# Scores first on TensorE, and column-order norms and coordinates fetched by DMA, in a fused attention and nearest-neighbour kernel

## The reference

```
q, k, v = projections of ctx; scores = q.k / 4 + mask bias   (inside each chunk of 64)
out = (softmax(scores) . v) W_out + b_out, times the mask, plus x, then normalised over the tokens
```

```
pd[n, m] = 2 p_n.p_m - |p_n|^2 - |p_m|^2 ; idx = top_k(pd, 30)
```

## Time and profile before

| | |
|---|---|
| Median of 3 runs | 6893.18 us (6890.46 to 6906.41) |
| Profiled execution, its own time | 6878.53 us |
| Its span in the trace | 6876.1 us |
| Mean granted TensorE clock | 0.894 |
| First stage, 0 to 5075 us: DVE busy | 4784.22 us |
| the same: PE busy | 4401.15 us |
| the same: POOL busy | 4301.12 us |
| the same: ACT busy | 3863.60 us |

### The profile page before, as it was taken

The page is one execution under the profiler, slowest core; times in us unless marked ns, Lnnn a source line. Parts: engine busy times, 40 slices in busy tenths (PEclk is TensorE's granted clock), DMA queues, the critical chain, the costliest instruction groups (busy, mean ns, idle before and its releaser), DMA issues. The chain is left out here.

```text
span 6876.1 us, 226732 instructions
## 1 busy us (share of the span) xinstructions
PE 5928.1 (86%) x84308; PEld 3577.8 (52%) x84308; DVE 6084.7 (88%) x8460; ACT 4455.0 (65%) x17112; POOL 4813.1 (70%) x4750
## 2 busy tenths in 40 slices
PE   8888888888888888888888888888857949999999
PEld 4555555545454555455545555555532327767776
DVE  7999999999999999999999999999976578777876
ACT  6777777777777777777777777777741543333333
POOL 6788888888888888888888888888870013333332
PEclk9988988889888888888888888889868979999999
DMA  1222222222222222222222222222223003332322
GB/s 34 75 71 84 80 78 71 78 71 78 71 87 80 78 72 83 80 77 71 77 71 77 72 75 92 73 76 83 70 95 72 0 22 85 84 92 80 91 80 76
DMA packets 245853, 508.79 MB, mean 74 GB/s; under 512 B 155868, under 2 KB 169436, under 8 KB 210780
## 3 DMA queue, kind: packets, MB, share of 16 engines
q1 hardware_dynamic: 244700, 493.37, 22.7%
HBM read 377.93 MB, written 65.01 MB: 64 GB/s over the span
## 5 line engine op out<-in xcount | busy, mean ns | idle before, releaser
L653 ACT ACTIVATE prob<-SC,row_max 128x64 f32<-128x64 f32 x6144 | 1830.1, 325 | 1080.2 <-DVE row_max L998 1037.2
L769 POOL TENSOR_TENSOR k_bd<-k_t,head_mask 128x512 f32<-128x512 f32 x1536 | 1700.6, 1128 | 7.4 <-POOL dist_row L747 4.5
L653 ACT ACTIVATION_READ_ACCUMULATOR prob<-SC,row_max 128x1 f32 x6144 | 1336.8, 218 | 0.0
L982 DVE FIND_INDEX8 nbr<-top,dist 128x8 uint16<-128x1024 f32 x1024 | 1234.5, 1217 | 0.0
L978 DVE MAX8 top<-dist 128x8 f32<-128x1024 f32 x1024 | 1192.8, 1205 | 12.2 <-DVE y_b L1021 9.9
L780 POOL TENSOR_TENSOR prob<-prob,row_rec 128x512 f32<-128x512 f32 x768 | 813.0, 1059 | 544.0 <-DVE row_rec L1006 543.3
L553 PE MATMUL SC<-k_bd,q_t 128*64 128x256 f32 x6144 | 923.8, 426 | 0.0
L980 DVE MATCH_REPLACE8 dist<-top,dist 128x1024 f32<-128x1024 f32 x768 | 923.4, 1206 | 0.0
L561 PE MATMUL PT<-ident,prob 128*128 128x128 f32 x3072 | 543.7, 304 | 401.5 <-ACT prob_t L660 396.2
L1780 DVE TENSOR_TENSOR d_oh_a<-lo,iota_a 128x4096 bf16<-128x4096 bf16 x256 | 583.8, 2291 | 245.8 <-PE DM L1632 245.6
L1673 ACT ACTIVATE dense<-DM 128x512 f32<-128x512 f32 x512 | 305.4, 597 | 756.5 <-PE DM L1632 756.2
(11 more groups left out here) (201 smaller groups left out, 10825.7 us busy)
## 6 DMA issues: line engine op xcount, KB each, us to landing
low_all<-low_scratch SPq DMA_DIRECT2D x256, 1024.0 KB, 5.1
placed<-compact SPq DMA_DIRECT2D x256, 192.0 KB, 3.8
ctx<-in_ctx SPq DMA_DIRECT2D x32, 512.0 KB, 4.1
mask<-in_mask SPq DMA_DIRECT2D x32, 512.0 KB, 7.3
xb<-in_x SPq DMA_DIRECT2D x32, 512.0 KB, 4.8
x_scratch<-xb SPq DMA_DIRECT2D x32, 512.0 KB, 5.0
y_scratch<-y_b SPq DMA_DIRECT2D x32, 512.0 KB, 6.6
d_x<-x_scratch SPq DMA_DIRECT2D x32, 512.0 KB, 5.0
```

What stands on the lines that cost most here:

```text
L653: last = act.activation(prob[:, s % 4, g * CHUNK:(g + 1) * CHUNK], SC[:, s % 2, g * CHUNK:(g + 1) * CHUNK], ACT.Exp, bias=row_max[:, s % 2 ...
L769: last = pool.tensor_tensor(k_bd[:, q % KEY_BUFS, ch, :].rearrange("p (h k) -> p h k", h=8), kk, hm, ALU.mult)
L982: last = dve.max_index(nbr[:, uu % BPB, t, k * 8:(k + 1) * 8], best, row)
```

## The change

Four edits, all in the first stage.

1. In PE's `step` the block of the scores moves ahead of the projections, the squares and the distance block. Nothing in the block itself changes.
2. The third use of the squares (h = 2, 16 matmuls) and its two copies on ACT go, with `perm3` and the semaphore `col_ready`. A batch then has 26 uses of `PJ` and not 27. ACT's copy of `PD` has no factor 2 any more, and `xcol` holds -|p|^2/2.
3. SP gets two new pieces. `columns_out` at step 17 waits for the two copies of `vrow`, stores one row of `vrow` (4 KB) to DRAM, and issues three loads that bring the coordinates from `ctx` in DRAM into `pts`, each of 1024 single values of 4 bytes spread over 128 partitions. `columns_in` at step 19 waits for the store and loads `xcol`, again 1024 single values. Both also run once before the first step.
4. ACT waits for `xcol` before the first `PD` copy of a batch, and before it overwrites `vrow` it waits for the store of the batch before. POOL's `split_row` waits for the `vrow` copies in place of `col_ready`, and `make_table` waits for the three loads.

```
-XX_AT = {8: (0,), 16: (1, 2)}
+XX_AT = {8: (0,), 16: (1,)}
+COLS_OUT_AT, COLS_IN_AT = 17, 19
...
+            def columns_out(i, ub):
+                copied(sp, i, ("xx", ub, 0))
+                alone(sp)
+                copied(sp, i, ("xx", ub, 1))
+                alone(sp)
+                sp.wait_ge(table_ready, at_least(i, START + i * BPB + ub - 1, START))
+                alone(sp)
+                sp.dma_start(dram["half_norms"][i * BPB + ub], vrow[0:1, :]).then_inc(cols_out, 16)
+                for c, row in enumerate((0, 2, 1)):
+                    sp.dma_start(pts[:, ub % BPB, :].rearrange("p (t c) -> p t c", c=3)[:, :, c],
+                                 dram["ctx"][i * BPB + ub][row].rearrange("(t p) -> p t", p=128), allow_slow_non_contiguous=True).then_inc(pts_in[ub % BPB], 16)
+
+            def columns_in(i, ub):
+                sp.wait_ge(cols_out, START + (i * BPB + ub + 1) * 16)
+                alone(sp)
+                sp.wait_ge(pd_copied, at_least(i, START + i * 2 * TILES + 2 * NT * (ub - 1), START))
+                alone(sp)
+                sp.dma_start(xcol[:, ub % BPB, :], dram["half_norms"][i * BPB + ub, 0].rearrange("(t p) -> p t", p=128), allow_slow_non_contiguous=True).then_inc(cols_in[ub % BPB], 16)
...
             def step(i, s):
+                ub = s // BSTEPS + 1
+                if real(i, s, STEPS) and real(i, ub, BPB):
+                    if s % BSTEPS == COLS_OUT_AT:
+                        columns_out(i, ub)
+                    if s % BSTEPS == COLS_IN_AT:
+                        columns_in(i, ub)
...
-                for t in range(NT):
-                    pe.matmul(bank[:, 8 + 3 * t:11 + 3 * t], ctx[:, ub % BPB, t * 128:(t + 1) * 128], perm3[:, :], start=True, stop=True)
-                for t in range(NT):
-                    last = pe.matmul(bank[:, t:t + 1], sq[:, t * 128:(t + 1) * 128], half_neg[:, 0:1], start=True, stop=True)
-                last.then_inc(pj_ready, 1)
...
-                act.activation(xcol[:, ub % BPB, :], bank[:, 0:32], ACT.Identity, scale=2.0).then_inc(free, 1)
-                copied(act, i, ("xx", ub, 2))
-                act.wait_ge(table_ready, at_least(i, START + i * BPB + ub - 1, START))
-                act.activation(pts[:, ub % BPB, :], xcol[:, ub % BPB, 8:32], ACT.Identity, scale=0.5).then_inc(col_ready, 1)
+                act.wait_ge(dist_row_ready, START + i * BPB + ub)
+                act.wait_ge(cols_out, START + (i * BPB + ub) * 16)
+                act.activation(vrow[:, h * HALF:(h + 1) * HALF], bank, ACT.Identity).then_inc(free, 1)
...
+                    if tt % NT == 0 and h == 0:
+                        landed(act, cols_in, i, u)
...
-                    pool.wait_ge(col_ready, START + i * BPB + ub + 1)
+                    copied(pool, i, ("xx", ub, 0))
+                    copied(pool, i, ("xx", ub, 1))
...
-                pool.wait_ge(col_ready, START + b + 1)
+                pool.wait_ge(pts_in[v % BPB], START + (i + v // BPB + 1) * 48)
```

More of the change, by code:

```diff
@@ L85, in uses_of_step @@
     return uses
-FIRST_USES = [("xx", 0, h) for h in range(3)] + [(what, 0, h) for what, h in PARTS]
+FIRST_USES = [("xx", 0, h) for h in range(2)] + [(what, 0, h) for what, h in PARTS]
 def number_uses():
@@ L105 @@
 NUMBER = number_uses()
-NUSE = BPB * 3 + PASSES * (len(PARTS) + 2)
+NUSE = BPB * 2 + PASSES * (len(PARTS) + 2)
 assert NUSE % 2 == 0 and len(NUMBER) == BODY * NUSE
@@ L183, in attention_and_neighbours @@
         mask_row = sb("mask_row", [3, BPB, T], BF16)
-        xcol = sb("xcol", [128, BPB, 32])
+        xcol = sb("xcol", [128, BPB, NT])
         q_t = sb("q_t", [128, 2, T])
@@ L246, in attention_and_neighbours @@
         squared = sem("squared")
-        col_ready = sem("col_ready")
+        cols_out = sem("cols_out")
+        cols_in = [sem(f"cols_in{u}") for u in range(BPB)]
+        pts_in = [sem(f"pts_in{u}") for u in range(BPB)]
         pool_split = sem("pool_split")
@@ L523, in step @@
                 u, w, p = s // BSTEPS, s // PAIRS, s % PAIRS
[L524 to L532, removed]
-                    pe.wait_ge(pd_copied, START + i * 2 * TILES + 2 * tt + h)
-                    pe.matmul(PD[:, :], pick3[:, :], dist_row[:, u, h * HALF:(h + 1) * HALF], start=True, stop=False)
-                    pe.matmul(PD[:, :], ctx[:, u, t * 128:(t + 1) * 128], ctx[:, u, h * HALF:(h + 1) * HALF],
-                              start=False, stop=True).then_inc(pd_ready, 1)
                 if real(i, s, STEPS):
@@ L555, in step @@
                     last.then_inc(scored, 1)
+                for name, rel, h in uses_of_step(i, s):
+                    if name == "xx":
+                        squares(i, rel, h)
+                    elif name != "y":
+                        projection(i, name, rel, h)
+                if real(i, s, STEPS) and s % SPAN < 2:
+                    tt, h = s // SPAN, s % SPAN
+                    t = tt % NT
+                    pe.wait_ge(dist_row_ready, START + i * BPB + u + 1)
+                    pe.wait_ge(pd_copied, START + i * 2 * TILES + 2 * tt + h)
+                    pe.matmul(PD[:, :], pick3[:, :], dist_row[:, u, h * HALF:(h + 1) * HALF], start=True, stop=False)
+                    pe.matmul(PD[:, :], ctx[:, u, t * 128:(t + 1) * 128], ctx[:, u, h * HALF:(h + 1) * HALF],
+                              start=False, stop=True).then_inc(pd_ready, 1)
                 r = s - LAG_T
@@ L1893, in constants @@
     out["pow_half"] = np.full((128, 1), -0.5, np.float32)
-    out["perm3"] = np.eye(128, dtype=np.float32)[:, [0, 2, 1]]
     out["turns"] = np.tile(np.array([SIGN_TIE, np.pi / 2], np.float32), (128, 1))
```

18 lines of the change are left out of this document (7 added, 11 removed).

## The result

The change makes the kernel faster, but by less than half of the forecast: 6843.64 us median (6840.01 to 6844.73, four runs) beside 6893.77 us of the kernel before, ratio 0.9923, 95% interval [0.9906, 0.994]. That is 50 us, where 107 were forecast. The profiled execution took 6844.73 us, its span is 6842.6 us.

A forecast was written before the change was run, and what follows sets the result against it. DVE, busy 4656 of 4900 us, was taken to bound the first stage. 31 crossings x 3.3 = 102 us, plus 5 for the start, made 107: 6893.2 - 107 = 6786 us, range 6740 to 6825.

The forecast's parts named there:

- the waits of steps 16 and 17: row_max's waits for scores, 2.85 and 1.88 us in the batch read, would go once PE drops the column matmuls.
- rival B: No measurable change: ACT gets PD and projections a score block later and takes the place; about 6893 us, chance 0.12.
- rival D: Slower: an idler PE runs more at half clock, DVE waits about 2 us a batch more; 6955 us, chance 0.08.
- rival E: Slower: column loads of 20 us each outlast their 57 us cover and ACT waits; about 7600 us, chance 0.03.
- The start: Batch 0: POOL's split_row and the projections move up by 6.6 us; 5 us taken once, bounds -30 to 6.6.
- rival A: DVE gets all of the 6.68 us a crossing, 207 us, as POOL's work closes up; 6681 us, chance 0.13.
- rival C: Half of the gain: POOL slower beside a busier DVE uses up the slack, or batches differ; 6840 us, chance 0.12.
- the sum of 107 us: First stage: 31 crossings at 3.3 us, 102 us, and 5 us for the start.
- The kept part of a crossing: Of 6.68 us a batch, 3.3 kept: POOL can come forward 2.9, slack is 0.4; new DVE wait 3.4 us.
- 0.4 us of slack at `low_all`: Mean slack between the load of low_all landing and hot of step 2, estimated from 9 of 28 batches that waited.
- DVE's busy time stays: Sign for the profile after: DVE's work is unchanged and its share of the first stage rises to about 97%.
- The wait of step 0: row_max's 1.95 us wait for scores would go, since scores no longer stand behind the distance block and POOL's last split_row part.

The follow-up runs named there:

- e2: The kernel after with the old order in the step (projections, distance block, then scores), so only the columns come by DMA: 6849.73 us, ratio 0.9932.
- e3: The kernel after plus 64 semaphore increments on TensorE, run once ahead of the third stage's loop: 6821.48 us, ratio 0.989.
- e7: e3 with SP's load of low_all for step 2 issued a step earlier, ahead of the result's stores: 6823.47 us, ratio 0.9909.
- e5: e3 with three of GpSimd's angle instructions in step 22 done on one column in place of 256: 6774.35 us, ratio 0.9838.
- e6: The control: e3 with GpSimd's residual addition of layer 0 (steps 9 and 13) on 2 of 512 columns: 6749.21 us, ratio 0.9805.
- e8: e3 with the second square, split_row and the column DMAs moved forward into steps 9 to 15: 6853.32 us, ratio 0.9953.
- e12: e10 with ScalarE's root moved to step 15 and GpSimd's product of root to step 16: 6727.51 us, ratio 0.9748.
- e1: The kernel before with only the scores moved ahead of projections and distance block; column matmuls stay on TensorE: 6880.8 us, ratio 0.9978.
- e4: The kernel after with the first stage's loop body written out twice, 7 turns in place of 14: 6869.58 us, ratio 0.9961.
- e10: e9 with the third stage's loop body written out twice, 7 turns in place of 14: 6769.99 us, ratio 0.9812.
- e9: e3 with VectorE's pair r2m and good moved from the end of step 13 to the end of step 14: 6827.38 us, ratio 0.9897.

## Why the prediction was right and wrong

The direction was right, and so were the readings that carry it. The columns gave 61 us of the first stage by themselves (e2, the start included); the waits of steps 16 and 17 went; the loads are hidden; ScalarE did not take the place (rival B), the clock of the first stage stayed at 0.89 (rival D), the loads landed in 2.4 and 4.5 us where 6 were taken (rival E). The start gave 7.0 us where 5 were taken. Full gain (rival A) did not come, for the reason that the prediction gave: GpSimd. The measured time is beside that of rival C (6840), but that is in good part luck: half of the gap is not of C's kind at all.

Three steps were wrong. Against the sum of 107 us the spans show 33.5 (and the medians 50): the crossings gave 60.8 in place of 102, the start 7.0 in place of 5, and the second and third stages took 34 us that the sum does not have.

**The sum has no term for the rest of the program.** "31 x 3.3 = 102 and 5 for the start" adds up the first stage alone; the third stage lost 32.6 us. The change takes instructions from TensorE's stream, and that moved the head of a loop that it does not touch to a place where each backward branch costs a second stop. e3 gives 30 us of it back with 64 instructions that only count up a semaphore. The Trainium skill, "Runtime: NRT & Kernel Launch" (Instruction fetch mechanics), says that instructions are fetched sequentially in blocks of 16 KiB, and that a taken branch to a target outside the window forces a fetch before execution goes on. The trace agrees with that for TensorE, which has 7,377 records in a turn of the first loop, and shows that the price depends on where the loop's head lies: 4.35 us at one head, 3.92 + 2.78 at another, 2.6 in the mean for the second. For the other engines it shows no such stop: ScalarE has 1,388 records in the same turn, and its branch takes under 0.1 us. That either stop is a fetch, and the second one that of the next block, is an inference from this rule; the runs show only the dependence on the place.

**The kept part of a crossing: 3.3 us forecast, 1.96 measured.** The mechanism was right ("it can be pulled forward only by what it waited"), its size was not. GpSimd had waited 2.0 and 2.9 us for the `row_rec` of steps 15 to 23 in even and odd batches, 2.45 in the mean; the prediction read 2.9 in one batch and let it stand for all. To this it added 0.4 us of slack at `low_all`, a chain that e7 showed to limit nothing.

What GpSimd gave can be read directly. The table has the time from its product of step 15 (`prob` times `row_rec`) to that of step 0 of the next batch, and from there to step 15, in us, means over 26 batches (the two make up a batch):

| | 15 to 0 | 0 to 15 |
|---|---|---|
| before | 67.6 | 91.3 |
| after, and e3 | 65.8 | 91.2 |
| e5 | 63.7 | 91.6 |
| e6 | 65.9 | 88.5 |
| e8 | 58.1 | 99.9 |
| e12 | 66.5 | 89.2 |

The change took 1.7 us from the first stretch and 0.1 from the second. In the first, the 2.45 us of waits are gone, but GpSimd's own work grew from 61.6 to 62.0 us and its other pauses by 0.3. This is the step that the sum had wrong: 0.45 for the batch that was read, 0.4 for work that grew, 0.3 for small pauses and 0.3 of slack that wasn't there, together 1.5 of the 3.3 us; with the first and last batches the mean over 31 crossings is 1.96. Should the missing 15 us of the one trace of before lie here, it would be some 2.4. The work grew by rival C's reason, GpSimd slower beside VectorE: two instructions that had taken 1.27 us in nearly every batch now fall beside VectorE's work and take 2.3 and 2.9 us, while the `k_bd` copies became shorter. One of them, in the kernel before and after (ns min/median/max):

```profile
L912 POOL TENSOR_TENSOR angle<-angle,degen x32: 1261/1270/1277, 460.3 to 5174.5; 128x512 f32<-128x512 f32 x32
L933 POOL TENSOR_TENSOR angle<-angle,degen x32: 1261/2346/2363, 445.6 to 5106.8; 128x512 f32<-128x512 f32 x32
```

"DVE's busy time stays" was wrong in the same way: it rose by 11.0 us. The prediction also expected `hot` to wait 30 us or more and `row_max` some 60 us, nearly all in step 1; `hot` waited 0.5 us, and `row_max` 118.1, most of it in step 0.

**The wait of step 0.** "The wait of 1.95 us goes" is true of the order alone (e1: 0.1 us left) and wrong for the whole change, where 1.8 us stand, more than the mean of 1.2 before. "That stands behind POOL's last `split_row` part" put the 3.26 us of idle time in front of PD down to GpSimd; the row itself says "<-issue": no semaphore. There the loop's branch ended last. Once the columns are gone as well, VectorE comes to step 0 early enough to meet the branch: all of the wait is in the 13 crossings in which the loop turns, 3.5 to 4.1 us each. In the end it cost nothing of its own (e4), since GpSimd set that place anyway. The batch that was read is one with a turn, too: the waits of steps 16, 17 and 0 come to 180 us over all batches and not to 31 x 6.68 = 207, and the first three steps of the program have 28 of the 226.2, so rival A's gain was put too high.

What the control taught goes beyond the prediction. The prediction treated VectorE's waits as the whole prize and its 4656 us of work as fixed. The path of a batch runs through GpSimd from step 15 to the `k_bd` of steps 0 to 2 (e5), and through VectorE and GpSimd's addition from there to step 14 (e6, e8, e12), so that a microsecond saved pays on whichever of them has its turn. The table says the same: e5 shortens the first stretch, e6 and e12 the second (e12 lengthens the first by 0.7 us), and e8, which moved work from the first to the second, won 7.7 us and lost 8.7. Why e6, with 2.5 us a batch, gained more than e12's 1.2 was not taken apart: it also shortens GpSimd's own work by some 2 us a batch.

## What to carry to other kernels

Before adding up the waits that a change removes on the busiest engine, follow each other engine through the same stretch and ask how far it can be pulled forward; that is the gain, and it should be averaged over all batches of the period, not read in one. "<-issue" in front of TensorE at a loop's edge can be the branch: look for its record before giving the time to a semaphore. Writing more turns out paid where that engine has the path (e10) and not where it hasn't (e4). After any edit compare the stages that the edit did not touch, since their loops move in the instruction stream. Look at the durations of one engine's identical instructions over a batch: where the same line takes 0.42 and 1.36 us, moving it pays without removing anything.

## What the runs showed of the hardware

- A backward branch stopped TensorE for 3.3 to 5.1 us at each turn; the branch records of the other engines are under 0.1 us long. Depending on the position of the loop's head a second stop of about 2.6 us followed (13 of them in the third stage); 64 semaphore increments ahead of the loop, 0.15 us each, removed it. Writing two turns out took 53 us from a stage of 1238 us (e9 to e10), 39 of them stops and 11 of them TensorE's busy time. The first matmuls behind a stop ran at a granted clock of 0.50 (eight transposes in 1.96 us, and in 1.07 at 1.00).
- A VectorE `tensor_scalar` from 128x512 fp32 in SBUF to SBUF took 0.42 us with GpSimd idle and 1.26 to 1.37 us beside a GpSimd `tensor_tensor`; the GpSimd copies beside it went from 2.05 to 2.40 us for two. The Trainium skill, "SBUF — State Buffer" (Who interferes with whom), says that such an instruction can take a pair of ports that VectorE and GpSimd share, for its whole length, and that the loser blocks until the other is done. The trace of e3 agrees: `r2m` ends at 2732.42, 0.28 us behind the end of GpSimd's addition at 2732.14, as if it had waited for it rather than run at a slower rate. VectorE's and GpSimd's timelines there:

```profile
2731.05 1.37 DVE L1084 TENSOR_SCALAR r2m<-r 128x512 f32<-128x512 f32 x1
2732.34 1.26 DVE L1085 TENSOR_SCALAR good<-r 128x512 f32<-128x512 f32 x1
```

```profile
2730.87 1.27 POOL L815 TENSOR_TENSOR y_b<-y_b,xb 128x512 f32<-128x512 f32 x1
2732.10 2.40 POOL L790 TENSOR_TENSOR k_bd<-k_t,head_mask 128x512 f32<-128x512 f32 x2
```

  e5 shows the waiting itself, on the other side. There GpSimd's L933 has two elements a partition, 0.20 us of work where VectorE does something else. Beside `hot` it takes 1.27 us, and in all 29 such batches it ends 0.05 us behind `hot`. The rows of VectorE and of GpSimd, and GpSimd's in a batch without `hot` beside it:

```profile
2773.25 1.27 DVE L1078 TENSOR_SCALAR low_all<-low_all,iota_p 128x4096 bf16<-128x4096 bf16 x1
2773.30 1.27 POOL L933 TENSOR_TENSOR angle<-angle,degen 128x2 f32<-128x2 f32 x1
...
4934.99 0.20 POOL L933 TENSOR_TENSOR angle<-angle,degen 128x2 f32<-128x2 f32 x1
```

- Loads of 1024 single 4-byte values (4 KB) landed in 2.4 us, and in 4.5 us where they read back the stored row of norms. The `own` loads of 32 KB in 256 pieces of 128 bytes take 3.0 us in the same run. By the count of pieces the new ones would have taken 10.8 (four times the 2.7 of the earlier trace rows); at this size the number of pieces hardly counted.
